# Half of the fc1 output's high parts made by ScalarE instead of VectorE

## The reference, cut to what matters

```python
xn = layernorm(x)                                  # x: 4 x 2048 x 512
s = recurrent_attention(xn)                        # q, k, v, a 128 x 128 memory with decay 0.99, Wo, a gate
h = layernorm(xn) * gamma + beta                   # 8192 rows of 512
w1 = (fc1_q - 128) * fc1_scales                    # 512 x 2048, one scale per group of 128 rows
y = silu(h @ w1 + fc1_bias)                        # 8192 x 2048
w2 = (fc2_q - 128) * fc2_scales                    # 2048 x 512
z = y @ w2 + fc2_bias
g = silu(xn + 0.5 * z)
out = x + s * g
```

## Time and profile before

| | |
|---|---|
| median of the runs | 1291.49 us (1291.27 to 1292.08) |
| profiled execution | 1291.07 us |
| its span, first to last instruction | 1289.2 us |
| mean granted TensorE clock | 0.986 of full speed |
| TensorE busy | 1204.1 us, 93% |
| VectorE busy | 1132.0 us, 88% |
| ScalarE busy | 906.9 us, 70% |
| GpSimd busy | 805.4 us, 62% |

### The profile page before, as it was taken

One profiled execution on the slowest core, in us unless ns is written; L12 is line 12 of the kernel. 1 busy time (PEld: TensorE's weight loads), 2 busy tenths in 40 slices (PEclk: granted clock), 3 DMA queues, 4 the chain that ended last, 5 costly groups with the idle time before them and its releaser, 6 DMA issues.

```text
span 1289.2 us, 18645 instructions
## 1 busy us (share of the span) xinstructions
PE 1204.1 (93%) x5900; PEld 608.0 (47%) x5900; DVE 1132.0 (88%) x1962; ACT 906.9 (70%) x1558; POOL 805.4 (62%) x766
## 2 busy tenths in 40 slices
PE   2678999999999999999999999999999999999993
PEld 1234454554545455454545545454554545455540
DVE  6778989889898988889898888989898898988986
ACT  6456677676777767777676877767687776768771
POOL 6258874848476594847659474765947476594624
PEclk9899999999999999999999999999999999999997
DMA  9511030211303021120302112030211203020101
GB/s 331 172 34 33 1 99 1 66 34 26 74 1 98 1 66 34 29 70 1 98 1 67 34 32 67 1 98 1 66 34 37 63 1 99 1 66 1 42 26 33
DMA packets 41620, 65.68 MB, mean 51 GB/s; under 512 B 11696, under 2 KB 11952, under 8 KB 41008
## 3 DMA queue, kind: packets, MB, share of 16 engines
q1 hardware_dynamic: 41232, 64.36, 18.4%
q10 hardware_dynamic: 288, 0.08, 0.0%
HBM read 47.59 MB, written 16.81 MB: 50 GB/s over the span
## 4 chain that ended last, share of the span: by engine, by line
PE 77%; DVE 11%; issue 5%; ACT 3%; POOL 3%; DMA 1%; SPq 0%; DVEq 0%; POOLq 0%; ACTq 0%
PE blk L466 28%; PE blk L484 27%; PE side L427 10%; DVE blk L722 5%; PE side L451 4%; DVE y_split L713 2%; PE side L443 2%; DVE y_split L708 1%; PE side L410 1%; DVE g_lo L692 1%; PE side L444 1%; PE side L445 1%; PE side L436 1%; POOL g_rows L1004 1%; ACT blk L603 1%
## 5 line engine op out<-in xcount | busy, mean ns | idle before, releaser
L722 DVE TENSOR_TENSOR blk<-blk,ratio_rows 128x512 f32<-128x512 f32 x960 | 644.9, 690 | 88.9 <-PE blk L484 85.3
L603 ACT ACTIVATE blk<-blk,ratio 128x512 f32<-128x512 f32 x768 | 508.1, 666 | 228.5 <-PE blk L466 218.6
L466 PE MATMUL blk<-h_split,q_sb 128*128 128x512 f16 x2048 | 613.8, 382 | 10.2 <-issue 4.9
L484 PE MATMUL blk<-w_sb,y_split 128*128 128x512 f16 x2048 | 610.6, 380 | 6.5 <-DVE blk L722 4.3
L484 PEld LDWEIGHTS blk<-w_sb,y_split 128*128 128x128 f16 x2048 | 199.4, 98 | 253.5 <-DVE blk L722 14.1
L466 PEld LDWEIGHTS blk<-h_split,q_sb 128*128 128x128 f16 x2048 | 196.3, 98 | 223.9 <-issue 36.3
L610 ACT ACTIVATE y_full<-blk,par,last 128x512 f32<-128x512 f32 x256 | 201.3, 786 | 112.4 <-PE blk L466 112.3
L713 DVE SCALAR_TENSOR_TENSOR y_split<-y_full,up,y_split 128x512 f16<-128x512 f32 x256 | 218.8, 855 | 0.0
L1016 POOL CAST h_split<-h_full 128x512 f16<-128x512 f32 x64 | 52.9, 826 | 251.5 <-ACT h_full L565 251.5
L708 DVE TENSOR_SCALAR y_split<-y_full,up 128x512 f16<-128x512 f32 x256 | 159.4, 623 | 5.0 <-ACT y_full L610 5.0
L1004 POOL TENSOR_SCALAR g_rows<-xt,mv,gs 128x512 f32<-128x512 f32 x64 | 141.5, 2218 | 0.1
(11 more groups left out here) (144 smaller groups left out, 1019.6 us busy)
## 6 DMA issues: line engine op xcount, KB each, us to landing
xt<-in_x SPq DMA_DIRECT2D x64, 256.0 KB, 4.7
x_again<-in_x SPq DMA_DIRECT2D x256, 64.0 KB, 1.9
out<-z_rows SPq DMA_DIRECT2D x256, 64.0 KB, 1.7
w_sb<-in_q SPq DMA_DIRECT2D x4, 1024.0 KB, 13.8
ratio_rows<-ratio_dram SPq DMA_DIRECT2D x4, 1024.0 KB, 7.6
y_split<-in_q SPq DMA_DIRECT2D x1, 1024.0 KB, 10.5
h_split<-in_q SPq DMA_DIRECT2D x1, 1024.0 KB, 12.7
z_rows<-in_q SPq DMA_DIRECT2D x1, 1024.0 KB, 14.6
```

The lines of the kernel that those rows point to most:

```text
L466: mm = pe.matmul(blk[J % 2][:], q1_sb[:, g, j // 4, w, j % 4 * P:(j % 4 + 1) * P], a[:, c % 2, g, :], start=(g == 0 and n == 0), stop=(g = ...
L484: mm = pe.matmul(blk2[:, i, :], y[:, J % Y_RING, rows], w2_sb[:, j, part, :], start=(j == 0 and n == 0), stop=(j == FB - 1 and n == len(te ...
L603: act.activation(blk[J % 2][:], blk[J % 2][:], ACT.Copy, scale=ratio1[:, at:at + 1]).then_inc(blk_scaled, 1)
L722: dve.tensor_tensor(blk2[:, i, :], blk2[:, i, :], ratio2_rows[:, j, :], ALU.mult).then_inc(blk2_scaled, 1)
```

## The change

ScalarE makes the high halves of the odd blocks. It does so one slot behind its SiLU, right after that slot's rescale, with a Copy activation that reads `y_full` and multiplies by `up_y`. VectorE makes those of the even blocks as before, and all low halves. `y_low` of an odd block now waits for a semaphore of ScalarE. `up_y` is handed to ScalarE by a semaphore of its own, which a one-column copy on VectorE raises ahead of the loop; ScalarE waits for it at the first odd block.

```diff
-        y_hi_done = sem("y_hi_done")
+        y_hi_done, y_hi_odd_done = sem("y_hi_done"), sem("y_hi_odd_done")
         y_lo_done = sem("y_lo_done")
+        y_scale = sem("y_scale")
...
+            def odd_y_high(J):
+                wait(act, blk2_done, NT * (J - Y_RING + 1))
+                if J == 1:
+                    act.wait_ge(y_scale, 1)
+                act.wait_ge(silu_done, J + 1)
+                act.activation(y_hi[:, J % Y_RING, :], y_full[:, J % 2, :], ACT.Copy, scale=up_y
+                               ).then_inc(y_hi_odd_done, 1)
+
...
                     else:
                         silu(at[0])
+                if (at := fc1_step(G - YHIGH_LAG) if G >= YHIGH_LAG else None) and at[1] == KC - 1 and at[0] % 2:
+                    odd_y_high(at[0])
...
             def y_low(J):
-                dve.wait_ge(y_hi_done, J + 1)
+                if J % 2:
+                    dve.wait_ge(y_hi_odd_done, J // 2 + 1)
+                else:
+                    dve.wait_ge(y_hi_done, J // 2 + 1)
...
+            dve.tensor_copy(branch_end[:], up_y).then_inc(y_scale, 1)
+
             for G in range(SLOTS):
...
-                if (at := fc1_step(G - YHIGH_LAG) if G >= YHIGH_LAG else None) and at[1] == KC - 1:
+                if (at := fc1_step(G - YHIGH_LAG) if G >= YHIGH_LAG else None) and at[1] == KC - 1 and at[0] % 2 == 0:
                     y_high(at[0])
```

## The result

The kernel after takes 1293.88 us, the median of 13 runs (1292.79 to 1295.74), against 1290.63 us for 13 runs of the kernel before (1289.26 to 1292.08). The ratio is 1.0025, with a 95% interval of 1.0017 to 1.0034: slower by 3.25 us. The profiled execution took 1294.64 us (span 1292.8). That is 3.57 more than the profiled execution of before, at nearly the same granted clock (0.988 against 0.986).

What follows compares the result with a forecast made beforehand. VectorE (masks for reads) and ScalarE (SiLUs for fc1) both hold TensorE up, at different places. Per chunk 0.89 + 0.47 - 0.50 - 0.45 = +0.41 us, times 14 +5.7, less 1.1 and 0.8: +3.8, 1295.0 us; range 1289 to 1300.

Steps and rivals of the forecast that it cites:

- The copy's price: One copy on ScalarE: about 0.7 us long, holding it for 0.61 us (called s), bounds 0.52 and 0.67.
- A: Slots 52 to 0: two copies add 1.22 us on ScalarE, slack 0.33, so TensorE loses 0.89 per chunk at slot 0.
- B: Slots 27 to 32: 0.14 us is free behind the SiLU of slot 30, so the copy of slot 28 costs 0.47.
- C: Read of slot 11 loses 0.84 us; without slot 4's y_high ahead of its mask it gains 0.50 (0.40 to 0.84).
- D, E: Reads of slots 23 and 35: losses of 0.15 and 0.30 us go, as y_highs of slots 20 and 28 leave VectorE.
- The five copies at nothing: Copies of slots 4, 12, 20, 36 and 44 are covered and cost nothing; uncovered, up to 0.61 us each.
- Fourteen times: Chunks 1 to 14: the per-chunk change of +0.41 us counts 14 times, giving +5.7 us.
- First chunk, last chunk and tail: Outside chunks 1 to 14: first chunk -1.1 us, last chunk nothing in sum, tail -0.8 us from two y_highs less.
- y_low waits: Rival: y_low of odd blocks waits for late ScalarE, gains C to E are lost, 13.3 us on top, 1308 us; chance 0.09.
- No change to be measured: Rival: the difference stays within 0.2% (2.6 us), 1293 to 1294 us, where s is 0.58 or C 0.59; chance 0.30.
- VectorE's relief wins: Rival: read of slot 11 stops waiting and the copy is as short as the gate SiLU; -4.7, 1286.4 us; chance 0.13.
- Every copy counts: Rival: none of the eight copies per chunk is covered on ScalarE; +27, 1318 us; chance 0.03.

Runs made afterwards that it cites:

- the second run: Against the kernel before, only the copy of slot 28 goes to ScalarE, the other high halves stay on VectorE; 1293.19 us in one run.
- the five copies: Against the kernel before, only the copies of slots 4, 12, 20, 36 and 44 go to ScalarE; 1281.22 us, ratio 0.9916.
- the last one: Copies of slots 4, 12, 20, 36, 44 plus 7 and 31, and a few in first and last chunk, on ScalarE; 1272.1 us, ratio 0.9854 against before.

## Why the prediction was right

It said 1295.0 us, slower; the median is 1293.88. Against the profiled execution it said +3.8, and the two profiled executions differ by 3.57, the medians by 3.25. Most of what remains is the base: the three runs known then had a median of 1291.49, the 13 known now 1290.63. The interval starts at 1.0017, so a difference just under 0.2% isn't excluded, while no change is.

- **The copy's price.** The estimate from the gate SiLU and the copy of wo_sb was 0.7 long and 0.61 to the next start; measured 0.71 and 0.61. The Trainium skill's page "ScalarE: Activation LUTs", section "What ACT_TABLE_LOAD costs", states 186 ns plus 0.833 ns per element, 93 more for a column operand and an overlap of 93; by that it would be about 706 ns, and 613 to the next start (an estimate), and the trace agrees.
- **A, slots 52 to 0.** Predicted 0.89, measured 0.87 (0.50 + 0.45 at slots 56 and 63, 0.16 more at slot 0, 0.25 less at slot 59). The prediction looked at slot 0 alone. The loss spreads over three waits, but as ScalarE works without a gap, their sum is what it lacks.
- **B, slots 27 to 32.** Predicted 0.47, measured 0.47, shown alone by the second run.
- **C, the read of slot 11.** Predicted 0.50, measured 0.50, in part by luck: the step took the y_highs of slots 52 and 60 to be caught up behind the qkv job, but 0.1 of it comes with them, and that of slot 4 is worth 0.39, just under the lower bound.
- **D, E.** Predicted 0.45, measured 0.45; with the copy of slot 28 alone the read of slot 35 is freed, and with the five copies that of slot 23.
- **The five copies at nothing.** Right: with these alone the kernel is faster by 10.3 us (1281.22 against 1291.49), and a second copy in each shows how much cover was left.
- **Fourteen times.** The steady period holds 13 times, in chunks 2 to 14. Chunk 1 took 77.13 us before and grew by 0.1 only. So where the sum had 5.7, chunks 1 to 14 give 5.1.
- **First chunk, last chunk and tail.** From slot 0 of the last chunk to the end 0.75 is gained (predicted 0.8), but not as the sum had it: the tail behind slot 63 gives 0.50, and the last chunk, which was to come to nothing, 0.25. Its read of slot 23 lost 0.74 before, not 0.15, and loses nothing after; B and a wait of 0.33 behind the copy of slot 52 take part of that back. The first chunk was 1.3 shorter (predicted 1.1), but its length lies between 95.7 and 99.0 us over the versions without following the copies: 99.0 with the copy of slot 4 alone and 97.4 with that of slot 28 alone, neither with a copy in slots 52 and 60. This term isn't shown. The 0.6 more ahead of chunk 0, where the sum had nothing, isn't explained either: over the versions, all with the same column copy, this stretch takes 35.9 to 37.4 us.

In the steady period the parts came out as forecast. In the total, the 0.6 us that the sum had too much for chunks 1 to 14 and the 0.5 that it took off too much for the rest nearly cancel: that much of the agreement is luck.

Of the rivals, *y_low waits* falls: `y_low` has no idle time ahead of it. *No change to be measured* is the nearest: 1293.88 lies in its 1293 to 1294 us, as the base came out 0.86 lower. But its condition (s of 0.58 or C of 0.59) did not come, and the interval leaves no change out. *VectorE's relief wins* falls with a read of slot 11 that still loses 0.33 and a hold of 0.61. *Every copy counts* falls with the five free ones. The Trainium skill's rule for multiplications (page "ScalarE: Activation LUTs", section "Rules for kernel authors"), taken literally, would have made all of the versions slower; the last one moves seven of sixteen to ScalarE in most chunks and is the fastest. The gains at the reads are there, and they are paid back in the two stretches where ScalarE ends last.

## What to carry to other kernels

Moving work from one busy helper to another is priced place by place: at each, ask which of the two TensorE waits for next, and how long the receiving engine is idle before that. Move the instances whose donor is late and whose receiver has a gap, and leave the others. The average busy shares barely tell such versions apart, while the period of the loop does: within one trace its 13 repeats agree to 0.02 us.

## What was not expected of the hardware

VectorE's remaining 128 y_highs average 705 ns, where the 256 of before average 623. Taken one by one from 210 to 1185 us of the traces, they fall into two groups. Of 208 before, 156 took 0.47 to 0.50 us and 52 took 0.63 to 1.52; of 104 after, 65 took 0.47 to 0.48 and 39 took 0.87 to 1.52. So the mean rose because three in eight of those that stay are long, instead of one in four. Every long one began while GpSimd had a 128x512 instruction under way. Meeting GpSimd alone is not enough: beside a 128x4 instruction a y_high took at most 0.50, and 38 (before) and 26 (after) of the short ones began inside a 128x512 one too, 13 of them 0.03 us behind its start and the others with at most 0.16 us of it left. One long pair in the kernel before, GpSimd and VectorE at slot 20 (start us, us, instruction):

```profile
387.36 1.27 POOL L1067 TENSOR_TENSOR z_rows<-z_rows,s_rows 128x512 f32<-128x512 f32 x1
```

```profile
387.74 1.18 DVE L708 TENSOR_SCALAR y_split<-y_full,up 128x512 f16<-128x512 f32 x1
```

The y_high ends 0.29 after GpSimd's instruction (388.92 against 388.63), where one that finds GpSimd idle takes 0.48. The Trainium skill's page "SBUF — State Buffer", section "Who interferes with whom", says that VectorE in a mode that uses both of its port pairs, which it lists `tensor_scalar` as able to enter if its operands allow, and GpSimd exclude each other, and that the first to issue keeps the shared pair for its whole instruction. The pair agrees with it in the order of the ends. The 13 short ones that began 0.03 us behind a GpSimd instruction don't fit it, if the rows have the order right. No row shows the mode and no run tested it, so the cause is argued only.

ScalarE's 128 copies do not spread like that: 0.709 to 0.770 us, over the whole run.
